# The first six low halves of a two-layer kernel move from GpSimd to VectorE

## The reference, cut to what matters

```python
xn = layernorm(x)
gate_out = xn @ (gate_t * gate_s[:, None]).T        # 1024 x 1792
up_out   = xn @ (up_t   * up_s[:, None]).T
hidden   = silu(gate_out) * up_out
ffn      = hidden @ (down_t * down_s[:, None]).T    # 1024 x 512
x = x + attn_branch(xn) + ffn
```

## Time and profile before

| what | value |
|---|---|
| median of 3 runs | 305.62 us (303.92 to 306.13) |
| the profiled execution's own time | 305.49 us |
| its span, first to last instruction | 303.6 us |
| TensorE matmul busy | 291.7 us, 96% |
| VectorE busy | 175.8 us, 58% |
| ScalarE busy | 118.4 us, 39% |
| GpSimd busy | 159.2 us, 52% |
| mean granted TensorE clock | 0.977 |

### The profile page before, as it was taken

The page is one execution under the profiler, slowest core; times in us unless marked ns, Lnnn a source line. Parts: engine busy times, 40 slices in busy tenths (PEclk is TensorE's granted clock), DMA queues, the critical chain, the costliest instruction groups (busy, mean ns, idle before and its releaser), DMA issues.

```text
span 303.6 us, 4378 instructions
## 1 busy us (share of the span) xinstructions
PE 291.7 (96%) x1573; PEld 194.3 (64%) x1573; DVE 175.8 (58%) x270; ACT 118.4 (39%) x197; POOL 159.2 (52%) x184
## 2 busy tenths in 40 slices
PE   6888989999999999999999999989999999999995
PEld 4785547665565657556565655646577888788784
DVE  3784796565725784684545745678887622333303
ACT  1552345453634132444635535223045730146500
POOL 4878259995391311155474284630467585047650
PEclk9795899999999999999999999999999999999999
DMA  7999618108000212010110011210020000200003
GB/s 256 328 286 208 101 35 124 33 1 121 2 0 2 69 36 71 0 35 13 37 35 26 2 35 38 69 35 2 0 69 1 3 1 32 73 35 0 0 2 138
DMA packets 11749, 17.86 MB, mean 59 GB/s; under 512 B 848, under 2 KB 6224, under 8 KB 11728
## 3 DMA queue, kind: packets, MB, share of 16 engines
q1 hardware_dynamic: 6624, 12.49, 12.7%
q0 software_dynamic: 4960, 4.98, 10.1%
q10 hardware_dynamic: 144, 0.12, 0.1%
HBM read 20.46 MB, written 2.10 MB: 74 GB/s over the span
## 4 chain that ended last, share of the span: by engine, by line
PE 85%; POOL 6%; DVE 4%; issue 2%; DMA 1%; ACT 1%; DVEq 0%; POOLq 0%
PE bank L593 15%; PE bank L594 15%; PE bank L690 15%; PE bank L561 8%; PE bank L563 8%; PE bank L562 8%; PE bank L652 5%; PE bank L624 3%; PE bank L630 2%; PE bank L555 2%; DMA early<-in_params 1%; PE bank L643 1%; PE bank L642 1%; PE bank L615 1%; POOL root L1079 1%
## 5 line engine op out<-in xcount | busy, mean ns | idle before, releaser
L1162 POOL TENSOR_TENSOR hidl<-hid,hidh 128x512 f16<-128x512 f32 x28 | 33.3, 1189 | 47.8 <-ACT hidh L756 47.6
L593 PE MATMUL bank<-xh,gatew 128*128 128x512 f16 (+1 forms) x136 | 45.5, 353 | 2.6 <-ACT XT L785 1.4
L594 PE MATMUL bank<-xl,gatew 128*128 128x512 f16 (+1 forms) x136 | 45.4, 353 | 0.0
L593 PE MATMUL bank<-xh,upw 128*128 128x512 f16 (+1 forms) x136 | 44.8, 348 | 0.0
L594 PE MATMUL bank<-xl,upw 128*128 128x512 f16 (+1 forms) x136 | 44.8, 348 | 0.0
L690 PE MATMUL bank<-downw,hidh 128*128 128x512 f16 x112 | 42.5, 380 | 0.0
L690 PE MATMUL bank<-downw,hidl 128*128 128x512 f16 x112 | 42.4, 379 | 0.0
L1168 POOL TENSOR_TENSOR actl<-hid,acth 128x512 fp32r<-128x512 f32 (+1 forms) x22 | 28.7, 1307 | 25.9 <-ACT acth L763 25.7
L1079 POOL TENSOR_TENSOR root<-var,powers 128x4 f32<-128x4 f32 (+1 forms) x25 | 23.6, 949 | 23.5 <-DVE var L942 19.9
L830 ACT ACTIVATE silu<-bank,early 128x512 f32<-128x512 f32 x28 | 19.2, 687 | 41.1 <-PE bank L594 41.1
L1011 DVE SCALAR_TENSOR_TENSOR hid<-bank,early,silu 128x512 f32<-128x512 f32 x28 | 21.0, 751 | 19.8 <-PE bank L594 19.3
(11 more groups left out here) (158 smaller groups left out, 607.1 us busy)
## 6 DMA issues: line engine op xcount, KB each, us to landing
X<-in_x SPq DMA_DIRECT2D x8, 256.0 KB, 5.6
out_x<-X SPq DMA_DIRECT2D x8, 256.0 KB, 2.0
downw<-in_down POOLq DMA_DIRECT2D x2, 896.0 KB, 8.3
stage<-in_v SPq DMA_DIRECT2D x6, 256.0 KB, 2.6
stage<-in_mask SPq DMA_DIRECT2D x4, 256.0 KB, 7.0
upw<-in_up POOLq DMA_DIRECT2D x1, 1024.0 KB, 11.9
gatew<-in_gate POOLq DMA_DIRECT2D x1, 1024.0 KB, 12.5
stage<-in_weight SPq DMA_DIRECT2D x4, 256.0 KB, 2.6
```

What stands on the lines that cost most here:

```text
L593: pe.matmul(bank_of(key)[:, c], w, xh[b][:, k, c], start=(k == 0), stop=False)
L594: mm = pe.matmul(bank_of(key)[:, c], w, xl[b][:, k, c], start=False, stop=(k == KT - 1))
L1162: pool.tensor_tensor(hidl[:, n % FT, :], hid[:, n % UNITS, :], hidh[:, n % FT, :], ALU.subtract).then_inc(hid_lo, 1)
```

## The change

The low halves of units 0 to 5 are made by VectorE, each right behind the product of the next unit, and signalled by a semaphore of their own, `first_lo`. GpSimd leaves these six out, and its count `hid_lo` starts at unit 6, so all waits on it are six lower. The products of units 3 to 8 lose their wait for a low half of GpSimd, since the halves they would wait for stand earlier in VectorE's own queue.

```diff
+LOWS = 6
...
             def low_rank_down(b, i):
-                pe.wait_ge(hid_lo, n + 1)
+                pe.wait_ge(hid_lo, n + 1 - LOWS)
...
                         if t == 0:
                             wait_codes(pe, "down", f)
-                            pe.wait_ge(hid_lo, unit(b, f) + 1)
+                            if unit(b, f) < LOWS:
+                                pe.wait_ge(first_lo, unit(b, f) + 1)
+                            else:
+                                pe.wait_ge(hid_lo, unit(b, f) + 1 - LOWS)
...
                 elif kind == "up":                     # VectorE
-                    if n >= UNITS:
-                        dve.wait_ge(hid_lo, n - UNITS + 1)
+                    if n >= UNITS + LOWS:
+                        dve.wait_ge(hid_lo, n - UNITS + 1 - LOWS)
                     dve.wait_ge(silu_ready, n + 1)
                     wait_full(dve, step)
                     emit(dve.scalar_tensor_tensor(out=hid[:, n % UNITS, :], ...
+                    if 1 <= n <= LOWS:
+                        dve.wait_ge(hid_hi, n)
+                        emit(dve.tensor_tensor(hidl[:, n - 1, :], hid[:, (n - 1) % UNITS, :],
+                                               hidh[:, n - 1, :], ALU.subtract), first_lo)
...
                 elif kind == "hidden":                 # VectorE
-                    dve.wait_ge(hid_lo, n - UNITS + 1)
+                    dve.wait_ge(hid_lo, n - UNITS + 1 - LOWS)
...
                 elif kind == "up":                     # GpSimd
                     n = unit(step[1], step[2])
+                    if n < LOWS:
+                        continue
```

More of the change, by code:

```diff
@@ L393, in two_layers @@
         hid_ready = sem("hid_ready")
-        hid_hi, hid_lo = sem("hid_hi"), sem("hid_lo")
+        hid_hi, hid_lo, first_lo = sem("hid_hi"), sem("hid_lo"), sem("first_lo")
         h_full = [sem(f"h_full{b}") for b in range(NBLK)]
@@ L1013, in _ @@
                                                   op0=ALU.mult, op1=ALU.mult), hid_ready)
+                    if 1 <= n <= LOWS:
+                        dve.wait_ge(hid_hi, n)
+                        emit(dve.tensor_tensor(hidl[:, n - 1, :], hid[:, (n - 1) % UNITS, :], hidh[:, n - 1, :],
+                                               ALU.subtract), first_lo)
                 elif kind == "down" and step[3] == DPIECES - 1:
```

## The result

| kernel | runs | median us | lowest, highest |
|---|---|---|---|
| before | 20 | 305.79 | 303.92, 306.22 |
| changed | 20 | 306.73 | 305.97, 310.58 |

The ratio is 1.0045 with a 95% interval of 1.0027 to 1.0062: the changed kernel is about 0.45% slower. That is under the 1% named in the prediction and still clear of noise. The forecast of 305.7 was 1.0 us too low; the time lies in the stated range and 0.1 us outside the own range of the likeliest case. The profiled execution of the changed kernel took 306.29 us with a span of 304.4, so its span is 0.8 us above that of before.

What follows compares the result with a forecast made beforehand. TensorE, busy 291.7 of 303.6 us, was taken as the bound. From 305.49 us, minus 2.3 (part 1), plus 2.25 (part 2 at `win 1`) and 0.15 (part 3), gave 305.6, forecast as 305.7; range 303.9 to 308.0.

Steps and rivals of the forecast that it cites:

- likeliest case: Whole kernel: the forecast's own sum, 305.7 us, own range 304.8 to 306.6; chance 0.40.
- Part 1: GpSimd's queue before block 1's root: without low(0), transposes 1.16 us earlier; clock returns early, 2.3 us advance at `up 2`.
- Rival E: XN held by something else, such as low(0); part 2 covered by TensorE's order: 305.5 us, no change; chance 0.08.
- Part 2: VectorE's saturated stretch, 34.46 to 49.30 us: low(1) to low(3) enter and add 2.5 us net, bounds 1.3 to 3.4.
- Part 3: Low(5) behind the product of unit 6, before `low` and `w1`: 0.15 us lost, between 0 and 0.7.
- C: VectorE's queue up to `win 1` costs 2.25 us, clock returns as before, advance only 0.58: 307.3 us; chance 0.25.
- D: Clock falls again at TensorE's idle time around `t1` or before `win 1`: 307.1 to 310.7 us; chance 0.10.
- The rule on SBUF: VectorE instructions with two SBUF inputs and GpSimd SBUF reads exclude each other: part 2 costs 2.5 us, without it 2.16.

Runs made afterwards that it cites:

- the root first: Against the kernel before: all low halves stay on GpSimd, that of unit 0 issued behind the two roots with that of unit 1; 303.78 us, ratio 0.9946.
- part 1 alone: Against the kernel before: unit 0's low half leaves its place before GpSimd's root, either to VectorE (303.82 us) or behind the roots on GpSimd (303.78 us).
- units 0 to 2: Against the kernel before: only the low halves of units 0 to 2 go to VectorE, the others stay on GpSimd; 304.80 us, ratio 0.9991.
- unit 0 alone: Against the kernel before: only the low half of unit 0 goes to VectorE, those of units 1 to 5 stay on GpSimd; 303.82 us, ratio 0.9949.

## Why the prediction was right, and where it was off

**Part 1, the advance.** Foreseen: 1.16 us at the transposes, 2.3 us at `up 2`. The trace has 2.45 us at the product of unit 2, and the early return of the clock, on which half of it rested, is in the windows (29.9 instead of 33.35). XN came 0.3 us earlier than worked out: it starts 1.15 us behind the start of the root, where it was 1.52 before; no run says why. Rival E (XN held by something else) falls.

That 2.3 met 2.45 so closely is in part luck. Both numbers are for an execution whose clock had fallen at 23.1 us. The eight profiles of kernels without a low half in front of the root have the product of unit 2 at 31.6 to 33.6 us, the two with it at 34.46 and 35.05. In four of the eight the clock was still full when the transposes began and fell within 0.8 us (with the root first it is low from 30.2 to 33.6), so nothing returned early there. What does not hang on one execution is the median: the two experiments with part 1 alone took 1.9 us less than before.

**Part 2, the stretch.** This is the term that was mis-sized: 2.5 us foreseen, 18.03 - 14.84 = 3.19 measured, inside its bounds of 1.3 to 3.4. Item by item: three low halves at 0.72, as foreseen; low(2) beside W1l 0.38 more (0.5 foreseen); XN 0.51 saved (0.50); the cast 0.06 saved (0.4 foreseen): beside it now run GpSimd's load of down weights (39.11 to 40.20) and the first table, and with the tables moved away it still takes 0.67, with nothing of GpSimd's beside it 0.43 (units 0 to 2); the scan 0.48 lost (0.57); low(3) met nothing (0.2 foreseen). The centring was left out of the sum altogether: 1.70 instead of 0.96 us, 0.74 lost. The prediction followed GpSimd's queue only to the tables. The second W1l behind them had moved forward too, from 50.65 to 45.99, onto the centring. Had that been followed, the sum would have been 3.2 and the forecast 306.4. (The upper bound of 3.4 comes out of its own terms as 3.3, and it left out the 0.57 on the scan that the sum itself held.)

**What reached TensorE.** Foreseen: 0.58 before `t1`, and `win 1` 2.25 us late against the advanced TensorE. On that measure it is 2.45 + 0.56 = 3.01 us, for `win 1` begins 0.56 us later than before, where the sum had it 0.05 earlier. The whole stretch came through: 3.19 less some 0.18 in hand. The medians agree, with 2.9 us between the changed kernel and that with unit 0 alone. The idle times that the profile shows, 0.43 + 0.27 + 1.49 = 2.19 us, look like the 2.25 but are another quantity: each such stop also takes the overlap of a matmul with the next (a start every 0.22 us at a length of 0.38). By the starts that is 0.17 us more at `t1` and at `z`, and 0.46 at `win 1`. The wait before `z` was not named.

**Part 3** was small, as foreseen: 0.15, between 0 and 0.7. From the 32 products of `win 1` to `w1` the changed kernel takes 9.27 us, and so does the kernel with three low halves left out. With units 4 and 5 on GpSimd it is 8.94 to 8.98, in the six profiles of before and of such kernels. So the traces have 0.3 us, and `low` took 1.64 us from 58.52. With tables 1 and 2 late it is 8.94 again, though units 4 and 5 are on VectorE: `low` takes 0.69 us there. In the median it does not show.

**The rivals.** C (the queue outweighs the advance) is right in its mechanism and its place, at a price between the forecast's and its own: the clock did come back early and the advance was as in the forecast, but the queue was 0.7 us longer, so VectorE added more up to `win 1` (3.0) than the advance at `up 2` (2.45). D (a fall of the clock) was given 0.10 and 307.1 to 310.7: it happens in 3 of 20 runs of the changed kernel, at 310.2 to 310.6. That reading of those three runs rests on the trace of another kernel, with units 1 to 5 on VectorE, where such a fall is seen; none of the three was profiled. Their mean granted clock is the lowest of the twenty, 0.978 against 0.981 to 1.000, which fits. It does not prove it, for runs of before have 0.976 to 0.978 at 305 to 306 us. Runs above 309 us occur only in the three kernels whose profile has the wait of 1.48 or 1.49 us before `win 1`, and in none of the 72 runs of the six other kernels of the experiments, nor of before. It stays open why only some executions fall.

**The rule on SBUF.** By the Trainium skill ("SBUF — State Buffer", section "Who interferes with whom") VectorE instructions with two SBUF inputs and GpSimd instructions that read SBUF exclude each other. The rows agree: low(2) takes 1.07 beside W1l and 0.69 alone, the centring 1.70 beside W1l and 0.69 without it, while `xl` and the products, which read a bank, keep 0.69 and 0.75 everywhere. XN, which the prediction puts beside L969, has X as its only full tensor input, so its 1.06 us beside a low half is no case of this sentence of the page.

## What to carry to other kernels

An instruction whose result nobody wants soon can still stand on the path, by what is queued behind it; moving it behind the root in its own queue gave the whole gain. Giving it to another engine gave the same; the loss came with the five that went along. Before adding work to an engine, look for its stretches without idle time: there an instruction costs its length, less the meetings that it removes and plus those that it brings (0.3 us for the low half of unit 1, 2 us or more for that of unit 3). And when work leaves a queue, follow all that moves forward in it until the queues are in step again, for each piece can meet something new.

## What the runs showed of the hardware that I had not expected

A fall of TensorE's granted clock needs no long idle time: in the kernel with units 1 to 5 on VectorE it fell 0.8 us into the float32 products of `win 1`, behind 1.48 us of idle time, and came back 10.2 us later. The same idle time in the profile of the changed kernel left it at full clock. So it was with the 1.36 us in front of `gate 4`: with units 0 to 2 on VectorE it fell right behind them, from 39.25 to 42.7, and in none of the nine other profiles did it. Nor does a long idle time bring a fall each time: in the profile with unit 0 alone TensorE stood idle for 3.08 us before the transposes at 29.55 and the clock stayed full, where before and changed kernel were at half at 29 us. Part of the spread of each kernel's runs (303.0 to 304.8 with unit 0 alone) may come from there; that was not tested.

One low half on VectorE, the fourth, cost 1.6 to 1.9 us for 0.72 us of work, more than twice its length, for its leaving GpSimd let the tables and the second W1l start earlier, into VectorE's scan and centring. With the tables moved away, 1.4 us of the stretch came back.
